# Attention and LoRA kernel: where TensorE's query, output and key products stand beside a step's values product

## The reference

```python
q = (x @ wq).reshape(B, T, 32, 32)
k = x @ wk
v = x @ wv
scores = jnp.einsum('bqhd,bkd->bhqk', q, k) * scale
scores = jnp.where(causal, scores, -jnp.inf)
probs = softmax(scores)
out = jnp.einsum('bhqk,bkd->bqhd', probs, v).reshape(B, T, C) @ wo
```

## Time and profile before

| | |
|---|---|
| median of three runs | 3394.73 us (3392.26 to 3398.16) |
| the profiled execution: its time | 3394.95 us |
| its span, first to last instruction | 3393.2 us |
| TensorE matmul busy | 3229.2 us (95%) |
| VectorE busy | 2265.3 us (67%) |
| GpSimd busy | 2061.9 us (61%) |
| ScalarE busy | 1598.3 us (47%) |
| mean granted TensorE clock | 0.978 |

### The profile page before, as it was taken

The page is one execution under the profiler, slowest core; times in us unless marked ns, Lnnn a source line. Parts: engine busy times, 40 slices in busy tenths (PEclk is TensorE's granted clock), DMA queues, the critical chain, the costliest instruction groups (busy, mean ns, idle before and its releaser), DMA issues.

```text
span 3393.2 us, 45475 instructions
## 1 busy us (share of the span) xinstructions
PE 3229.2 (95%) x15976; PEld 1616.3 (48%) x15976; DVE 2265.3 (67%) x5974; ACT 1598.3 (47%) x3180; POOL 2061.9 (61%) x741
## 2 busy tenths in 40 slices
PE   7899999999999999999999999999999999999996
PEld 3444444455554455554444445444555444544443
DVE  4776677777778667774366667776776776677605
ACT  2334454445555455555333344444455554555552
POOL 1326676776666887777211176667667577678870
PEclk9999999999999999999999999999999999999998
DMA  3422111110101000001211211112010100011000
GB/s 115 113 60 63 50 51 35 49 40 29 51 23 57 23 23 29 29 23 38 63 51 51 79 44 40 39 38 63 23 57 23 38 17 23 23 38 53 8 1 25
DMA packets 133011, 144.03 MB, mean 42 GB/s; under 512 B 28200, under 2 KB 93736, under 8 KB 132784
## 3 DMA queue, kind: packets, MB, share of 16 engines
q1 hardware_dynamic: 132480, 140.72, 14.1%
q10 hardware_dynamic: 304, 0.41, 0.0%
HBM read 72.91 MB, written 16.78 MB: 26 GB/s over the span
## 4 chain that ended last, share of the span: by engine, by line
PE 69%; POOL 15%; DVE 7%; issue 5%; ACT 2%; SPq 2%; DMA 1%; POOLq 0%; ACTq 0%; DVEq 0%
PE ps L1463 12%; PE ps L1435 12%; POOL ds L708 11%; PE ps L1424 11%; PE ps L1566 11%; PE ps L1389 10%; PE ps L1476 3%; DVE mx L1037 2%; PE ps L1525 2%; POOL ds L705 2%; SPq L600 2%; ACT pr L804 1%; PE ps L1606 1%; PE ps L1620 1%; PE ps L1576 1%
## 5 line engine op out<-in xcount | busy, mean ns | idle before, releaser
L804 ACT ACTIVATE pr<-ps 128x512 f32<-128x512 f32 (+3 forms) x2560 | 1288.0, 533 | 1428.5 <-PE ps L1435 1064.3
L708 POOL TENSOR_TENSOR ds<-ds,pr 128x2048 f32<-128x2048 f32 (+1 forms) x360 | 1491.8, 4144 | 139.8 <-ACT pr L804 108.7
L1435 PE MATMUL ps<-qs,ks 98*128 98x512 f32 (+3 forms) x2560 | 1358.8, 539 | 38.7 <-DVE mx L1037 15.3
L1037 DVE TENSOR_REDUCE mx<-ps 128x1 f32<-128x512 f32 x1536 | 996.5, 680 | 391.1 <-PE ps L1424 385.1
L1424 PE MATMUL ps<-ks,qs 96*128 96x512 f32 (+3 forms) x2560 | 967.5, 390 | 54.2 <-ACT pr L804 23.5
L1435 PEld LDWEIGHTS ps<-qs,ks 98*128 98x128 f32 x2560 | 487.2, 191 | 664.2 <-issue 296.1
L1034 DVE CUSTOM_DVE_ANT_0 ps<-ps,mask_qk 128x128 f32<-128x128 f32 (+3 forms) x1024 | 489.2, 496 | 453.7 <-PE ps L1424 449.9
L1424 PEld LDWEIGHTS ps<-ks,qs 96*128 96x128 f32 x2560 | 491.6, 194 | 337.5 <-ACT pr L804 137.8
L1463 PE MATMUL ps<-pr,vs 128*32 128x512 f32 (+3 forms) x5120 | 617.6, 551 | 6.9 <-POOL pr L715 6.9
L1389 PE MATMUL ps<-xT,wq_sb 128*128 128x512 f32 x1024 | 527.8, 607 | 4.4 <-ACT zs L831 1.9
L1566 PE MATMUL ps<-wo_sb,ao 128*128 128x512 f32 x896 | 466.3, 609 | 0.7 <-DVE q L1026 0.4
(11 more groups left out here) (162 smaller groups left out, 1949.9 us busy)
## 6 DMA issues: line engine op xcount, KB each, us to landing
qs<-q SPq DMA_DIRECT2D x762, 64.0 KB, 2.0
wq_sb<-in_L_attn_wq_dram SPq DMA_DIRECT2D x64, 512.0 KB, 4.0
t<-in_L_attn_x_dram SPq DMA_DIRECT2D x32, 512.0 KB, 6.5
xr<-in_L_attn_x_dram SPq DMA_DIRECT2D x28, 512.0 KB, 4.5
out_dram<-xr SPq DMA_DIRECT2D x28, 512.0 KB, 4.8
wo_sb<-in_L_attn_wo_dram SPq DMA_DIRECT2D x8, 512.0 KB, 5.5
qs<-mT SPq DMA_DIRECT2D x252, 4.0 KB
xT<-in_L_attn_x_dram SPq DMA_DIRECT2D x4, 512.0 KB, 5.3
```

The lines of the kernel that those rows point to most:

```text
L708: nc.gpsimd.tensor_tensor(ds[:, :, c0:], ds[:, :, c0:], this, ALU.add).then_inc(added, 1)
L804: nc.scalar.activation(pr[:, k % NS, g, c0:], ps[:, PM + EXP_PLACE[head(n, t, g)] % NPM, c0:], ACT.Exp, scale=SCALE).then_inc(exp_done, 1)
L1037: nc.vector.tensor_reduce(found, seen, AX.X, ALU.max).then_inc(mx_done, 1)
L1435: last = nc.tensor.matmul(ps[:, bank, c0:], ks[0:STK + 2, c:c + P], qs[0:STK + 2, n % NS, g, c0:], start=True, stop=not by_mask)
```

## The change

Two rules of TensorE's order are changed, and nothing on the other engines. First, `beside_values` goes over the finished table of a unit: in a slot that takes a step's values, everything from the first `q`, `proj`, `kv` or `early` on is taken out and put at the head of the next slot's pieces, except in the last slot of a unit. Second, `values_at` puts the values of `zeroed` steps in slot `g == 3` in place of `g == 2`; those of a unit's last step stay in slot 2 of the next unit. The values slots are worked out with the new places.

```diff
--- before.py
+++ after.py
@@ -88,6 +88,15 @@
     def zeroed(n, t):
 
         return cols(n, t)[1] and qb_of(n) > 0
+
+    def values_at(n, j):
+
+        t, g = j // GH, j % GH
+        n_, t_ = (n, t - 1) if t else (n - 1, steps(n - 1) - 1)
+        if n_ < 0:
+            return []
+        after = 1 if not zeroed(n_, t_) else 2 if t_ == steps(n_) - 1 else 3
+        return [(n_, t_)] if g == after else []
 
     def item(n, s):
         c, qt = s // TB, s % TB
@@ -181,7 +190,23 @@
         if n + 1 < UN:
             for who in ("PE", "ACT", "SP"):
                 put(rows_slot(n + 1), who, "rows", n + 1)
-        return found
+        return beside_values(n, found) if engine == "PE" else found
+
+    def values_slot(n, j):
+
+        return len(values_at(n, j)) > 0
+
+    def beside_values(n, found):
+
+        kept, late = {}, []
+        for j in range(slots(n)):
+            here, late = late + found.get(j, []), []
+            if values_slot(n, j) and j + 1 < slots(n):
+                cut = next((x for x, s in enumerate(here) if s[0] in ("q", "proj", "kv", "early")), len(here))
+                here, late = here[:cut], here[cut:]
+            if here:
+                kept[j] = here
+        return kept
 
     def post(at, blk, N):
 
@@ -1645,8 +1670,7 @@
                     scores(n, t, g)
                     for m in items(n, j):
                         max_scores(*m)
-                    n_, t_ = (n, t - 1) if t else (n - 1, steps(n - 1) - 1)
-                    if n_ >= 0 and g == (2 if zeroed(n_, t_) else 1):
+                    for n_, t_ in values_at(n, j):
                         values(n_, t_)
                     for stage, *a in at.get(j, []):
                         if stage == "q":
```

## The result

| | before | after |
|---|---|---|
| median (lowest to highest), us | 3394.21 (3392.26 to 3398.16) | 3359.32 (3355.06 to 3366.78) |
| profiled execution: time, span, us | 3394.95, 3393.2 | 3359.56, 3357.8 |
| TensorE busy, and the rest of the span, us | 3229.2, 164.0 | 3199.9, 157.9 |
| mean granted TensorE clock | 0.978 | 0.985 |

The ratio is 0.9897, 95% interval 0.9885 to 0.9909: the change saves 35 us, 1.0%.

A forecast was written before the change was run, and what follows sets the result against it. TensorE, busy 95% of the span, was taken as the bound, so only its waits could change. Terms -6.0 - 1.1 + 1.3 + 0.8 = -5.0 us against 3394.95 us gave 3389.8 us, range 3380 to 3397 us.

The forecast's parts named there:

- Masks, -6.0: Diagonal steps of units 30, 31 and the last: later values remove TensorE's waits for GpSimd's mask, -6.0 us (bounds 0 and -9.6).
- In the other 40-odd units with a diagonal no such wait shows, and the later values cost nothing there: Units with a diagonal where TensorE shows no wait for the mask: placing values one slot later was put at nothing.
- Fifth rival: A half-clock stretch of TensorE comes or goes, up to 2.7 us each, two or more needed; 3384 to 3400 us, 5%.
- Products out of the values slot, -1.1: Eight units with unit 26's pattern: exps behind the output product's copy start 0.14 us earlier each, -1.1 us; elsewhere 0.
- Last matmuls moved, +1.3 and +0.8: Product ends lose cover for waits on copies: units 33 to 36 +1.3 us, units 5 and 37 +0.8 us.
- The 110 us: Estimated TensorE loss to full PSUM banks: weight-load waits for maxima and exps, less 0.24 us each, 87 + 23 us.
- first rival: Smoothing products is worth more, as waits for full banks come in bursts behind values plus product; likeliest 3382 us, 24%.
- the bound of 38 us: Most that moving products could gain, if 221 of 640 steps lost their share of the estimated full-bank waits: -38 us.
- a wait given back: On the diagonals TensorE comes earlier but waits for exps instead of the mask; 3393 to 3397 us, 14%.
- late copies: At sixteen product ends ScalarE's copies come late and hold exps, 14 us less the mask's 6; about 3403 us, 9%.

## Why the prediction was wrong

It was wrong in size: the change is 1.0% faster, where I gave no change that can be told the higher chance.

*Masks, -6.0: right.* The later values in units of 64 slots alone gave 6 us; units 30 and 31 are 2.1 and 2.3 us shorter where 2.1 and 1.8 were forecast, the last unit 3.3 where 1.4 was, and there are 2.64 us between the values in unit 30 where 2.7 was forecast.

*"In the other 40-odd units with a diagonal no such wait shows, and the later values cost nothing there": this step failed,* and it is the larger part of the miss. The later values in units of 32 slots give 21 us. I had looked for waits for the mask alone. With the later values the stretches at half clock of units 11, 14, 16, 46, 47 and 48 are gone, 5.7 us long on average over the kernel (148/26). The later values' own saving of waits there is small, 4.0 us of idle time; the clock gives up to 16. By what the later values keep the clock up stays open. They shorten the wait in unit 46 from 0.82 to 0.25 us, but in unit 47 it grows from 0.74 to 0.97 us (0.99 with the later values in 32 slots alone), and the stretch behind it is gone all the same.

*Fifth rival, a stretch at half clock comes or goes, 5%: right in kind, wrong in number.* I priced one stretch properly at 2.7 us, and wrote that two or more would be needed. Before has 26. Ahead of nearly all of them TensorE waits, from 0.25 us up to several us. Those of units 11, 14, 16 and 46 to 48 sit in units with the same pattern, and the edit takes them away together, not one by one. I had read the clock in one window; reading it in windows over the whole span, which the profile of before allowed, would have shown 148 us of such time. I treated as chance what hangs in good part on the edit.

*Products out of the values slot, -1.1: the place was right, the size wasn't.* I took 0.14 us (1243.97 - 1243.8 = 0.17 by its own figures) from one place in unit 26 and multiplied by eight. The eight units are shorter by 6.8 us, six of them by 0.93 to 1.01 each, and with the products alone by about the same (6.3). In unit 26 the waits of TensorE fell at three places: from 0.31 to 0.02 us (slots 8, 9), from 0.91 to 0.53 (slots 20, 21) and from 0.17 to 0 (slot 25), 0.84 us. I had costed one place of three, and only through the copy; the bank waits behind it I had left at their old length. Elsewhere I had put it at 0, and that failed too: units 10 to 13 and 42 to 45 lose 0.5 to 1.0 us each against the later values alone, 4.9 us together, and that eats most of the gain.

*Last matmuls moved, +1.3 and +0.8: the first right, the second half.* Units 33 to 36 are 0.34, 0.36, 0.38 and 0.35 us longer, forecast 0.33. Unit 5 is 0.36 longer. Unit 37 is 1.08 us shorter, but this is the clock: before has 3.4 us at half clock in it and after none. The later values alone, with the key product where it stood, have none either and are 1.40 us shorter, so the move costs 0.32 us here as well.

*The 110 us.* I meant them as the sign by which the first rival would show, and they rose to 147 us while the kernel got faster. They were no measure, and neither was the bound of 38 us taken from them. The first rival's size was met and passed, but not by its mechanism: the smoothing of products is worth 5 us. The rivals of a wait given back and of late copies didn't come: units 30 and 31 keep their 4.3 us, and the query product's matmuls wait 3.1 us for ScalarE's copies where it had been 1.9, far from 5 us more.

"TensorE: Matmul & The Clock Gate" of the Trainium skill, under A second HAM failure mode: psum-queue depth-cycling, describes a kernel in which brief idle times between groups of matmuls, from cycling through PSUM banks, let the clock swing between its two levels, and finds its median matmul at the full rate, with the loss in throughput. The trace agrees: a ring of five banks, waits mostly of 0.2 to 1 us, 26 stretches at half clock, and a median of 592 ns for the query product's matmuls, next to their shortest of 590. That the median doesn't show it doesn't mean that single matmuls don't: the longest of these took 1167 ns, and the same eight values matmuls are passed in 1.86 us in a stretch and in 0.99 outside it.

## What to carry to other kernels

In a kernel whose TensorE is 95% busy, read the granted clock in windows over the whole span first, and ask for each stretch at half clock what stands ahead of it; an edit that takes a stretch away is worth up to half of it, several times the short wait ahead. Don't read off the length of one wait whether a stretch will follow (0.74 us had one, 0.97 us at the same place had none). Price an edit of the order at every place of a unit at which it acts, not at the one that was found first, and don't use sums of weight-load idle as a measure, since an edit of the order changes whom they are put down to. Whether it is the clock can be tested cheaply: a few matmuls by zeros into an accumulating bank at the waiting places, with the order left alone. Compare such runs unit by unit, since stretches elsewhere in the kernel move the total by several microseconds.

## What the hardware showed that I had not expected

- A TensorE that hardly waits can still lose clock. It was busy 135.24 of 140 us, with single waits under 1 us, and had a mean granted clock of 0.90; with 24 matmuls by zeros more it had 1.00, and the kernel took 9.5 us less. Idle time alone doesn't say it: after was busy only 133.31 of the 140 us, and had 1.00.
- More work can be faster, up to a point. 24 zeros at six places gave 9.5 us; 267 at 91 places gave 11 us and a clock of 0.990, for TensorE was busy 19 us longer and 69 us of half-clock time were left.
- Stretches at half clock move. Profiles of kernels that differ in a few slots have 18 to 26 of them (148 to 103 us), some in units far from the edit; a local gain of 1.4 us (units 33 to 36) was lost this way in one run, and one of 6.4 us in another. Executions of one and the same kernel differ in it too (the products alone: 3381 to 3398 us at clocks from 0.982 to 0.977). That sets how well a change of order in such a kernel can be predicted at all: 5 us either way is my estimate, the distance of those two runs' medians (3363.26 and 3358.21).
